# First attention of a three-layer sequence kernel: VectorE's first maxima ahead of the heads' normalisation, TensorE's transposes of heads and of the next input later

## What is computed

```
h = layer_norm(x, ln1_g, ln1_b)
q, k, v = split(h @ w_qkv.T)            # 16 heads of 16
scores = q @ [k_before, k_now].T * scale    # blocks of 128 queries, 256 keys
scores = where(band, scores, -inf)      # key j in i+1 .. i+128
attn = softmax(scores) @ [v_before, v_now]
x = x + attn @ w_o.T
h = layer_norm(x, ln2_g, ln2_b)
x = x + gelu(h @ mlp_w1.T + mlp_b1) @ mlp_w2.T + mlp_b2
```

## Time and profile before

| | |
|---|---|
| median of 3 runs | 1790.45 us (1790.11 to 1791.4) |
| span of the profiled execution, first to last instruction | 1791.1 us (no other time of that execution is given) |
| TensorE busy | 1731.2 us, 97% |
| VectorE busy | 1494.1 us, 83% |
| ScalarE busy | 1197.5 us, 67% |
| GpSimd busy | 1080.0 us, 60% |
| mean granted TensorE clock | 0.994 |
| chain of waits, by engine | TensorE 84%, VectorE 9%, ScalarE 3%, issue 3% |

### The profile page before, as it was taken

The page is one execution under the profiler, slowest core; times in us unless marked ns, Lnnn a source line. Parts: engine busy times, 40 slices in busy tenths (PEclk is TensorE's granted clock), DMA queues, the critical chain, the costliest instruction groups (busy, mean ns, idle before and its releaser), DMA issues.

```text
span 1791.1 us, 43798 instructions
## 1 busy us (share of the span) xinstructions
PE 1731.2 (97%) x15424; PEld 1496.0 (84%) x15424; DVE 1494.1 (83%) x3797; ACT 1197.5 (67%) x3088; POOL 1080.0 (60%) x1060
## 2 busy tenths in 40 slices
PE   6999999999999999999999999989999999999997
PEld 4778777789998888888887888878888888888886
DVE  6888988868878898888987678789898898967776
ACT  6999988854445787877876334358787877743332
POOL 3676556534434778778773455377878777634343
PEclk9999999999999999999999999999999999999999
DMA  3111211032322111111112434331111111131221
GB/s 107 38 37 38 67 44 31 26 107 75 108 63 99 48 41 54 44 52 51 44 43 71 147 105 126 100 103 41 52 44 55 41 54 47 31 102 56 82 82 36
DMA packets 139812, 116.03 MB, mean 65 GB/s; under 512 B 10584, under 2 KB 138848, under 8 KB 138848
## 3 DMA queue, kind: packets, MB, share of 16 engines
q1 hardware_dynamic: 139616, 113.53, 20.5%
HBM read 75.74 MB, written 37.75 MB: 63 GB/s over the span
## 4 chain that ended last, share of the span: by engine, by line
PE 84%; DVE 9%; ACT 3%; issue 3%; POOL 0%; DMA 0%; SPq 0%; DVEq 0%; POOLq 0%; ACTq 0%
PE psum L567 17%; PE psum L569 17%; PE psum L568 17%; PE psum L906 6%; PE psum L874 5%; PE psum L887 5%; PE psum L682 3%; PE psum L664 3%; PE psum L848 3%; ACT a_probs L1718 2%; PE psum L920 2%; PE psum L617 1%; DVE a_neg_max L1211 1%; DVE psum L1209 1%; PE psum L654 1%
## 5 line engine op out<-in xcount | busy, mean ns | idle before, releaser
L1837 ACT ACTIVATE b_probs<-masked,neg_max 128x256 f32<-128x256 f32 (+1 forms) x512 | 250.6, 494 | 124.3 <-DVE neg_max L1343 124.3
L1343 DVE CUSTOM_DVE_ANT_0 masked<-psum,mask 128x256 f32<-128x256 f32 (+1 forms) x512 | 177.3, 412 | 75.9 <-PE psum L874 75.9
L567 PE MATMUL psum<-wa_hi,b_h_hi 128*128 128x512 f32 (+1 forms) x576 | 233.8, 406 | 6.9 <-DVE wa_lo L1138 3.9
L568 PE MATMUL psum<-wa_lo,b_h_hi 128*128 128x512 f32 (+1 forms) x576 | 214.0, 372 | 0.0
L569 PE MATMUL psum<-wa_hi,b_h_lo 128*128 128x512 f32 (+1 forms) x576 | 214.0, 372 | 0.0
L567 PE MATMUL psum<-g_h_hi,wm_hi 128*128 128x512 f32 (+1 forms) x480 | 190.5, 397 | 2.7 <-POOL g_h_lo L2121 1.6
L2070 POOL TENSOR_TENSOR g_in<-g_in,minus_half 128x16 f32<-128x16 f32 x64 | 188.2, 2940 | 4.5 <-DVE g_in L1295 4.5
L568 PE MATMUL psum<-g_h_lo,wm_hi 128*128 128x512 f32 (+1 forms) x480 | 189.3, 394 | 0.0
L569 PE MATMUL psum<-g_h_hi,wm_lo 128*128 128x512 f32 (+1 forms) x480 | 189.2, 394 | 0.0
L1458 POOL TENSOR_TENSOR g_in<-g_z,g_in 128x512 f32<-128x512 f32 x62 | 79.8, 1287 | 143.4 <-DVE g_in L1289 138.2
L567 PE MATMUL psum<-wm_hi,u_hi 128*128 128x256 f32 x576 | 164.3, 285 | 0.1
(11 more groups left out here) (169 smaller groups left out, 5644.0 us busy)
## 6 DMA issues: line engine op xcount, KB each, us to landing
x_mid<-y_out SPq DMA_DIRECT2D x96, 128.0 KB, 1.7
rope_in<-in_rope SPq DMA_DIRECT2D x64, 128.0 KB, 2.2
x_res<-x_state SPq DMA_DIRECT2D x64, 128.0 KB, 2.2
g_in<-x_mid SPq DMA_DIRECT2D x32, 256.0 KB, 3.8
g_old<-x_state SPq DMA_DIRECT2D x16, 512.0 KB, 4.0
out_x<-g_fin SPq DMA_DIRECT2D x15, 512.0 KB, 2.9
w_raw<-in_w_mlp_b SPq DMA_DIRECT2D x2, 2154.0 KB, 8.8
x_in<-in_x SPq DMA_DIRECT2D x32, 128.0 KB, 2.2
```

The source lines that it names most:

```text
L567: nc.tensor.matmul(out, a_hi, b_hi, start=first, stop=False)
L568: nc.tensor.matmul(out, a_hi, b_lo, start=False, stop=False)
L1343: ins = nc.vector.tensor_tensor_reduce(out[:, at], src[:, at], (mask if now else mask0)[:, at], -1.0, BIG, ALU.add, ALU.min, neg_max[:, r, ...
L1837: ins = nc.scalar.activation(out, src, ACT.Exp, bias=neg_max[:, r, k:k + 1], scale=-1.0, accum_out=row_sum[:, n % 2, 4 * r + k:4 * r + k + 1])
```

## The change

Three programs are reordered, and no instruction is added or removed. VectorE takes `maxima(4 * s)` ahead of `normalize_heads(s - 2)`. TensorE takes `project_qk(s + 1)` and `transpose_probs(4 * s)` ahead of `transpose_o(s - 2)` and `transpose_z(s + 2)`. ScalarE takes `exponentials(4 * s)` ahead of `o_high(s - 2)`, which stays ahead of `copy_twice(s + 1, 1)`.

```
@@ TensorE
                 if a_chunk(s - 1):
                     transpose_probs(4 * s - 1)
-                if a_chunk(s - 2) and s < NCH - 1:
-                    transpose_o(s - 2)
                 if s == NCH - 1:
                     pe.wait_ge(S["kt_lo"], NCH)
                     pe.wait_ge(S["qt_ready"], NCH)
                     pe.wait_ge(S["o_ready"], 2 * (NCH - 3) + 2)
                     pe_mlp(pe, MLP_A, MA, None, opening="z")
-                if s == -1:
-                    project_qk(0)
-                if a_chunk(s + 2):
-                    transpose_z(s + 2)
-                if a_chunk(s + 1) and s > -1:
+                if a_chunk(s + 1):
                     project_qk(s + 1)
                 if a_chunk(s):
                     transpose_probs(4 * s)
+                if a_chunk(s - 2) and s < NCH - 1:
+                    transpose_o(s - 2)
+                if a_chunk(s + 2):
+                    transpose_z(s + 2)
                 if a_chunk(s - 1):
                     values(s - 1, 1)
@@ VectorE
+                if a_chunk(s):
+                    maxima(4 * s)
                 if a_chunk(s - 2) and s != NCH + 1:
                     normalize_heads(s - 2)
                 if a_chunk(s):
-                    maxima(4 * s)
                     maxima(4 * s + 1)
@@ ScalarE
+                if a_chunk(s):
+                    exponentials(4 * s)
                 if a_chunk(s - 2) and s != NCH - 1:
                     o_high(s - 2)
-                if a_chunk(s):
-                    exponentials(4 * s)
                 if a_chunk(s + 1):
                     copy_twice(s + 1, 1)
```

## The result

The changed kernel takes 1837.14 us (median of 4 runs, 1834.29 to 1839.64), the kernel before 1790.93 us beside it: a ratio of 1.0256, 95% interval 1.0244 to 1.0268. The forecast was 1834.5, in a range of 1822 to 1850. The profiled execution took 1837.88 us, with a span (first to last instruction) of 1836.1; the span before was 1791.1.

A forecast was written before the change was run, and what follows sets the result against it. It took a chain of 7.43 us TensorE plus 3.37 us VectorE and ScalarE to bound each step. 29 × 1.50 = 43.5 us, with the ends 44.0, took the span 1791.1 to 1835.1, median 1834.5; range 1822 to 1850.

The forecast's parts named there:

- What bounds a step: In steps of the first attention, 7.43 us of TensorE and 3.37 us of VectorE and ScalarE make the period of 10.80.
- VectorE's move saves nothing: Maxima of round 0 ahead of normalised heads still wait for the scores; at most 0.03 us saved, counted as nothing.
- TensorE's move costs 0.44 us behind 277.87: Four transposes, formerly hidden, follow the first probabilities' exponentials; values start 0.44 us later, a cost per step taken alone.
- ScalarE's round trip decides: `o_high` waits for eight transposes behind the first exponentials, holding `copy_twice` and the next exponentials: 1.50 us a step, 29 steps.
- The rule on queues: ScalarE's queue is strictly first in, first out, so nothing passes the waiting `o_high`: delay 1.50 us, otherwise 0.44 us.
- VectorE has room, barely: VectorE's work from `gain_bias` through the statistics ends 0.24 us before the next maxima are due, so it stays hidden.
- The ends: Outside the 29 steps: 0.1 us for steps 0 and 1 together, and 0.4 us for step 31.
- Only TensorE's part costs: Rival, 6%: slack covers ScalarE's wait in the steps, leaving 0.44 us in each of 29, 13 us: 1803 us.
- Faster: Rival, 4%: early scores let each step's chain lose 0.69 us, with 0.44 given back; 7 us gained: 1783 us.
- The clock: Rival, 6%: TensorE's clock falls at the steps' pauses; 2004 us if at each, 1868 us if a fifth of that.

The follow-up runs named there:

- the run with k's copy first: The changed kernel with ScalarE's `copy_twice(s + 1, 1)` moved ahead of `o_high(s - 2)`: 1831.30 us.
- two tries: The changed kernel with `o_high` behind `gain_bias`, split of o and statistics later: 1817.02 us; then `o_high` also behind `copy_probs`, the split between later maxima: 1824.77 us.
- VectorE's part alone: The kernel before with only `maxima(4 * s)` moved ahead of `normalize_heads(s - 2)`, TensorE and ScalarE in their old order: 1848.39 us.
- the run with `o_high` last: The changed kernel with `o_high` behind k's copy and the exponentials of round 1, `gain_bias` still waiting for it: 1860.15 us.

## Why the prediction was right

- *What bounds a step* (7.43 us of TensorE, then VectorE and ScalarE) held: the chain of the changed kernel goes the same way round, with the new pieces in it.
- *VectorE's move saves nothing*: right. The masking copy starts 0.80 us after the first scores (274.42, 275.22), it was 0.78 (257.70 less 256.92), and undoing the move changes neither time nor steps. That it costs nothing holds only with the other two parts: alone it costs 57 us.
- *TensorE's move costs 0.44 us behind 277.87*: right in size; the values start 1.02 us after the transposes of probabilities (278.89), before 0.58.
- *ScalarE's round trip decides*: right. The eight transposes take 1.09 us (277.87 to 278.96), as forecast. The sum per step was 1.50 us and the chip took 1.56 (45.16 over 29). The one hand-over that was mis-sized is that from the transposes to `o_high`: 0.10 us (278.96 to 279.06), not 0.03. `copy_twice` follows 0.28 us later, the exponentials 0.48, the scores 0.05 after their end: as forecast. In the 29 steps ScalarE is idle for 36.0 us ahead of line 1739, 1.24 each; in the same steps of the kernel before it never waited there. Two experiments bear it out from both sides: without TensorE's late transposes the same place costs 0.20 us, and with one of the queued instructions taken out from behind the wait, and VectorE given room, 0.48 us come back.
- *The rule on queues.* The Trainium skill (TensorE: Matmul & The Clock Gate, "Architectural detail: the array is 16× 32×32, not 1× 128×128") has ScalarE as strictly first in, first out. The trace now agrees: k's copy, whose input TensorE had finished at 276.76 + 0.40 = 277.16, started at 279.34, behind the waiting `o_high`, with ScalarE idle for 1.24 us. In the run with k's copy first it started 1.01 us after the exponentials (272.30, 273.31), without a wait.
- *VectorE has room, barely*: right, 0.20 us where 0.24 was forecast, and it mattered for the experiments more than for the sum. Four of them moved the loss from ScalarE to VectorE or to TensorE's wait for a bank.
- *The ends*, 0.1 us for steps 0 and 1 and 0.4 for step 31, are the part that came out by luck: all before step 2 took 1.45 us less in the profiled execution, and step 31 and all after it 1.29 us more. Together that is 0.2 us less, where 0.5 more was forecast, although neither end came out as forecast. The first half of step 31 is 2.1 us longer (398.51 to 405.65, before 354.80 to 359.84). TensorE waits 1.76 us there for normalised heads before the MLP's first transposes, which was forecast as a wait of 0.4; and the matmuls that follow then run at about half the rate, with a grant of 0.52 from 402.30 to 405.65 (0.77 over the step, where it was 0.90):

```profile
401.60 1.48 PE L1022 MATMUL psum<-ident,g_z 128*128 128x128 f32 x8 [1.76 <-DVE mask L1216]
```

With VectorE's order undone there is no such wait (the same transposes take 1.04 us), and the first half of the step takes 5.05 us. So the 2.1 us are VectorE's part. What is left of them at the end is not settled: from step 31 to the end the executions with VectorE's old order take 1434.0 to 1437.5 us, so 1.3 us is within what single executions differ by.
- *The rivals.* "Only TensorE's part costs" fell: 46 us, not 13. It would be near the truth only with every other wait out of the way, and two tries did not get there (26 and 33 us). "Faster" fell with VectorE's order undone. The clock did not fall in steps 2 to 30, but this is in part luck. The prediction argued from the share of a step for which TensorE is busy, 85%. VectorE's part alone has about that share (10.74 of 12.46 us, 86%, in a step that kept the clock) and lost the clock in seven others. The row that the prediction took for full clock, 22 to 34, is not clean either: it says 1.00, but its first matmuls, those of lines 568 and 569, start at 22.13 and 22.55, 0.42 us apart, about the distance seen above at a grant of 0.52.

## What to carry to other kernels

A move that takes work off the chain of waits gains only if what comes up next is earlier; here the scores ended only 0.07 us before the normalised heads (257.66, 257.73), so the chain went through the scores for the same time. Where an engine hands to another and its own next instruction waits for the answer, the price is the whole round trip, with what is queued behind the waiting instruction: here eight transposes, a rounding and a copy stood between two sets of exponentials that before had only the copy between them. When a late instruction is moved to help one queue, look at every buffer and bank that it frees: ScalarE's wait for the transposes, VectorE's full middle of the step, the copy of the probabilities and the split of o took each other's place here, one after the other.

## What was not expected of the hardware

- A hand-over from TensorE to `o_high` took 0.10 us in every step read, and one from `o_high` to `gain_bias` 0.14 us (279.44 to 279.58), where others take 0.02 to 0.05. Both instructions wait for more than one semaphore, but so do the first exponentials, which start 0.02 us after the maxima (276.65, 276.67). The Trainium skill (Perfetto Trace Analysis, "Identifying Dependency Chains") says that an instruction that waits for several engines may have separate semaphore instructions put ahead of it. The trace has 32 of them on ScalarE's sequencer, 17 ns each, at line 1738, `o_high`'s wait for `xt_ready`, though both of its waits are for TensorE; one stands in the chain above at 279.00, between the transposes' end and `o_high`. What makes the rest of the 0.10 us was not tried.
- TensorE's clock went to the 1.2 GHz level in seven of 29 steps of VectorE's part alone, with a pause of 1.57 us in each step (grant 0.87 or 0.88 over those steps), and stayed at 2.4 GHz in the changed kernel's steps 2 to 30 with pauses of 0.72 and 1.04 us and about the same busy time (10.6 of 12.35 us against 10.7 of 12.46). The length of the pause does not explain it alone: the run with `o_high` last has a pause of 1.62 us and one of 0.72 in its steps, and its clock fell only once in 29 steps, around 341.5 to 345 us (grants of 0.93 and 0.95 over the two steps there). What tells the steps that lost the clock from the others is open.
